# The last stage of a four-stage kernel, moved in blocks of 512 tokens into the steps of the third stage

## What is computed

```python
x = x + ln(windowed_attention(ln(x)))      # first stage,  "a"
x = x + ln(attention_and_8_experts(ln(x))) # second stage, "b"
x = x + ln(state_space_layer(ln(x)))       # third stage,  "c"
x = x + ln(mlp(ln(x)))                     # last stage,   "d"

def state_space_layer(x):                  # runs along the 256 tokens of a sequence
    x_ssm, z = split(ln(x) @ W_in)
    x_ssm = silu(causal_conv4(x_ssm)); dt = softplus(x_ssm @ dt_w + dt_b)
    h_t = exp(dt_t * A) * h_(t-1) + dt_t * x_t * B_t;  y_t = h_t @ C_t
    return x + ((y + x_ssm * D) * silu(z)) @ W_out

def mlp(x):                                # 128 -> 512 -> 512 -> 512 -> 128
    h = silu(x @ w1) * (x @ w2)
    h = gelu(h @ h1); h = gelu(h @ h2)
    return h @ w3
```

## Time and profile before

| what | value |
| --- | --- |
| median of 3 runs | 1017.56 us (1017.52 to 1021.14) |
| profiled execution, its own time | 1019.39 us |
| its span from first to last instruction | 1017.6 us |
| PE busy | 854.1 us, 84% |
| DVE busy | 680.2 us, 67% |
| ACT busy | 556.4 us, 55% |
| POOL busy | 459.0 us, 45% |
| chain that ended last, PE's share | 23% |
| granted TensorE clock, mean | 0.843 of full speed |

### The profile page before, as it was taken

One profiled execution on the slowest core, in us unless ns is written; L12 is line 12 of the kernel. 1 busy time (PEld: TensorE's weight loads), 2 busy tenths in 40 slices (PEclk: granted clock), 3 DMA queues, 4 the chain that ended last, 5 costly groups with the idle time before them and its releaser, 6 DMA issues. The chain is left out here.

```text
span 1017.6 us, 21550 instructions
## 1 busy us (share of the span) xinstructions
PE 854.1 (84%) x8256; PEld 704.6 (69%) x8256; DVE 680.2 (67%) x1965; ACT 556.4 (55%) x1050; POOL 459.0 (45%) x781
## 2 busy tenths in 40 slices
PE   4888755789999999989587887887579999999994
PEld 4777644668888888767455576665458878788783
DVE  4888954757888887652399999999772180551712
ACT  3554522346667676646478877786354363542630
POOL 2876852323646454444467777867540020020201
PEclk9877855559999999977789877788589999999997
DMA  8200002000000000000000000000000000000000
GB/s 283 94 18 12 24 17 66 25 1 2 2 2 2 2 3 2 1 2 1 0 1 2 1 1 1 1 1 1 1 1 1 1 21 1 1 22 1 16 6 21
DMA packets 22149, 16.76 MB, mean 16 GB/s; under 512 B 2576, under 2 KB 20376, under 8 KB 21792
## 3 DMA queue, kind: packets, MB, share of 16 engines
q1 hardware_dynamic: 21040, 14.77, 4.7%
q10 hardware_dynamic: 1008, 0.63, 0.2%
HBM read 11.20 MB, written 4.19 MB: 15 GB/s over the span
## 5 line engine op out<-in xcount | busy, mean ns | idle before, releaser
L118 POOL TENSOR_TENSOR d_ln_ve<-d_ln_mv,eps 128x4 f32<-128x4 f32 x16 | 3.2, 200 | 228.7 <-DVE d_ln_mv L112 228.7
L1421 PE MATMUL ps<-h_h,wh_h 128*128 128x512 f32 x256 | 99.7, 389 | 0.0
L1423 PE MATMUL ps<-h_l,wh_h 128*128 128x512 f32 x256 | 99.6, 389 | 0.0
L1422 PE MATMUL ps<-h_h,wh_l 128*128 128x512 f32 x256 | 99.6, 389 | 0.0
L1500 PE MATMUL ps<-w_e,he 128*128 128x128 f32 x512 | 87.0, 309 | 3.7 <-ACT he L690 3.4
L690 ACT ACTIVATE he<-ps,pp 128x256 f32<-128x256 f32 x128 | 59.7, 472 | 43.6 <-PE ps L1423 38.1
L1500 PEld LDWEIGHTS ps<-w_e,he 128*128 128x128 f32 x512 | 76.9, 221 | 6.1 <-ACT he L690 5.4
L1434 PEld LDWEIGHTS ps<-mov,hbd 32*128 32x128 f32 x2048 | 78.1, 232 | 0.0
L1434 PE MATMUL ps<-mov,hbd 32*128 32x32 f32 (+1 forms) x2048 | 77.2, 308 | 0.0
L1388 DVE TENSOR_TENSOR d_y<-ps,w_s 128x512 f32<-128x512 f32 x8 | 5.5, 692 | 103.0 <-PE ps L1857 103.0
L1354 DVE TENSOR_TENSOR h_l<-hid,h_h 128x512 fp32r<-128x512 f32 x64 | 48.5, 771 | 31.3 <-ACT h_h L921 30.4
(11 more groups left out here) (286 smaller groups left out, 2614.8 us busy)
## 6 DMA issues: line engine op xcount, KB each, us to landing
x<-in_x SPq DMA_DIRECT2D x16, 128.0 KB
w_h<-in_w_h SPq DMA_DIRECT2D x2, 1024.0 KB, 8.2
x<-x SPq DMA_DIRECT2D x16, 128.0 KB, 1.8
xB<-x SPq DMA_DIRECT2D x32, 64.0 KB
out_x<-xB SPq DMA_DIRECT2D x32, 64.0 KB
w_m<-in_w_m SPq DMA_DIRECT2D x3, 256.0 KB, 5.8
xB<-in_w_e SPq DMA_DIRECT2D x1, 512.0 KB
w_e<-in_w_e SPq DMA_DIRECT2D x1, 512.0 KB
```

Source lines behind the costliest of these rows:

```text
L1421: pe.matmul(dst, a_h, b_h, start=start, stop=True, skip_group_check=True)
L1422: pe.matmul(dst, a_l, b_h, start=False, stop=True, skip_group_check=True)
L1423: return pe.matmul(dst, a_h, b_l, start=False, stop=True, skip_group_check=True)
```

## The change

The last stage runs in 8 blocks (b = 0 to 7) of 512 tokens, one lane. Its work is put into `step_c` on every engine. `block_of(n, behind)` gives the block that a step works on: a block enters in step 2b + 4 (its norm, its turned tiles, gate and up of m = 0), is in the middle in step 2b + 5 (gate and up of m = 1 to 3, hidden layer 1), ends in step 2b + 6 (hidden layer 2, last product), and leaves in step 2b + 7 (output norm, addition). So from step 5 on the steps alternate: odd ones have a middle (and from 7 on a leaving) block, even ones an ending and an entering block. Blocks 0 to 5 end inside the third stage; block 6 enters in step 16, and `tail()` does the rest of block 6 and block 7.

The blocks use PSUM banks 6 and 7 alone: gate and up of one m take both, a hidden layer alternates between them. For that the pair products go through banks 4 and 5 in two halves (`pairs(t, k)`, `terms(t, k)`, k = 0, 1), and the B and C projections go to bank 5 (BC = 5). The products of the second half follow in the next step, behind `terms(n, 0)`. Lanes are gone: `raw`, `gate`, `d_xh`, `h0_h` and so on exist once. The weights are split in steps 0 to 4 (two of ten pieces a step, ACT `weight_heads`, POOL `low_parts`). The output norm of the third stage is done one step earlier. In the tail, other banks are used too. Every matmul of the last stage is still made, as many as before.

The diff, cut to its core:

```diff
-        IN, DT, BR, STATE, PAIRS, BC = 0, 1, 2, 3, 4, 7
+        IN, DT, BR, STATE, PAIRS, BC = 0, 1, 2, 3, 4, 5
...
+        def block_of(n, behind):
+            return (n - behind) // 2 if n >= behind and (n - behind) % 2 == 0 and n <= NB else None
...
         @block.scalar
...
+            def hidden1(b, m):
+                act.wait_ge(m_h1_ps, nth(b, m))
+                if m >= 2:
+                    act.wait_ge(m_h1, nth(b, m - 2))
+                chain.link(act.activation(raw[m % 2][:, :], ps[:, hidden_bank(b, 0, m), :], ACT.Gelu, scale=vec("h1_s", m)))
+                act.activation(h1_h[:, m, :], raw[m % 2][:, :], ACT.Copy).then_inc(m_h1_high, 1)
...
             def step_c(n, have):
...
                 if have(1):
                     log_part(n + 1)
+                if middle is not None:
+                    gated(middle, 0)
                 if have(0):
                     skip_path(n)
+                if middle is not None:
+                    high0(middle, 0)
+                    gated(middle, 1)
+                if ending is not None:
+                    hidden2(ending, 0)
...
+                if ending is not None:
+                    hidden2(ending, 2)
+                    hidden2(ending, 3)
+                if entering is not None:
+                    turned_tokens(entering)
                 if have(2):
                     silus(n + 2)
+                if middle is not None:
+                    gated(middle, 2)
...
+                    gated(middle, 3)
+                    high0(middle, 3)
                 if have(1):
                     decays(n + 1)
+                if middle is not None:
+                    hidden1(middle, 0)
...
+            def tail():
+                gated(b, 0)
+                output_norm(NB - 1)
+                gated(b, 1)
...
         @block.vector
...
+            def raised(b, m):
+                dve.wait_ge(m_gate, nth(b, m))
...
+                dve.scalar_tensor_tensor(out=raw[m % 2][:, :], in0=ps[:, up_bank(b, m) + 1, :], scalar=vec("w2_s", m),
+                                         in1=gate[m % 2][:, :], op0=ALU.mult, op1=ALU.mult).then_inc(m_raw, 1)
...
             def step_c(n, have):
+                if entering is not None:
+                    tokens_in(entering)
                 if have(2):
                     conv_input(n + 2)
+                if leaving is not None:
+                    tokens_out(leaving)
+                if ending is not None:
+                    low1(ending, 2)
+                    low1(ending, 3)
                 if have(0):
                     decay_products(n)
                 if have(-1):
                     from_states(n - 1)
-                if have(0):
-                    terms(n)
+                if middle is not None:
+                    raised(middle, 0)
+                if have(0):
+                    terms(n, 0)
...
+                if leaving is not None:
+                    output_normed(leaving)
                 if have(0):
                     carried(n)
...
                 if have(1):
                     inputs_by_chunk(n + 1)
+                if middle is not None:
+                    low0(middle, 3)
+                if n >= 4 and have(-1):
+                    residual(n - 1)
+                if have(0) and n >= 4:
+                    states(n)
+                if entering is not None:
+                    tokens_low(entering)
+                if ending is not None:
+                    scaled(ending)
...
         @block.tensor
...
-            def pairs(t):
+            def pairs(t, k):
...
-                    pe.wait_ge(S["c_term"], t)
-                for g in range(4):
-                    last = pe.matmul(ps[:, PAIRS + g, 0:BC_AT], ones[heads(g), :], prod[l][heads(g), :],
-                                     start=True, stop=True)
+                    pe.wait_ge(S["c_term"], 2 * t + k)
+                for g in range(2):
+                    part = heads(2 * k + g)
+                    last = pe.matmul(ps[:, PAIRS + g, 0:BC_AT], ones[part, :], prod[l][part, :], start=True, stop=True)
...
+            def gate_and_up(b, m):
+                if m == 0:
+                    pe.wait_ge(S["d_xl"], b + 1)
+                    if b >= 1:
+                        pe.wait_ge(S["d_yr"], min(b, LAST - 1))
+                elif b < LAST - 1:
+                    pe.wait_ge(m_raw, nth(b, m - 1))
...
+            def hidden(b, w, m):
+                src_h, src_l, ready, done = ((h0_h, h0_l, m_h0, m_h1_ps), (h1_h, h1_l, m_h1, m_h2_ps))[w]
+                if m == 0:
+                    pe.wait_ge(ready, nth(b, HID - 1))
+                elif m >= 2 and b < LAST - 1:
+                    pe.wait_ge((m_h1_high, m_h2)[w], nth(b, m - 2))
...
             def step_c(n, have):
                 if have(1):
                     in_and_out(n + 1)
                     step_size(n + 1)
                 if have(2):
                     turned_input(n + 2)
                 if have(-1):
                     from_states(n - 1)
+                if ending is not None:
+                    hidden(ending, 1, 0)
+                if have(0):
+                    pairs(n, 1)
                 if have(1):
                     outputs_by_chunk(n + 1)
+                if middle is not None:
+                    gate_and_up(middle, 1)
                 if have(2):
                     convolved(n + 2)
+                if middle is not None:
+                    gate_and_up(middle, 2)
+                if ending is not None:
+                    hidden(ending, 1, 1)
                 if have(0):
                     chunk_weights(n)
                 if have(1):
                     inputs_by_chunk(n + 1)
+                if middle is not None:
+                    gate_and_up(middle, 3)
+                if ending is not None:
+                    hidden(ending, 1, 2)
                 if have(0):
                     chunk_states(n)
+                if middle is not None:
+                    hidden(middle, 0, 0)
                 if have(-1):
                     projected(n - 1)
+                if ending is not None:
+                    hidden(ending, 1, 3)
+                if entering is not None:
+                    tokens_turned(entering)
                 if have(1):
-                    pairs(n + 1)
+                    pairs(n + 1, 0)
+                if middle is not None:
+                    hidden(middle, 0, 1)
+                if ending is not None:
+                    last_product(ending)
                 if have(0):
                     turned_states(n)
+                if middle is not None:
+                    hidden(middle, 0, 2)
+                    hidden(middle, 0, 3)
+                if entering is not None:
+                    gate_and_up(entering, 0)
```

More of the change, by code:

```diff
@@ L32 @@
 ITER = NB // 2
-ITER_MLP = NB // 4
 PP = {}
@@ L625, in _ @@
                     products(0)
[L626 removed]
+            for n in range(0, NB + 1):
                 step_c(n, within(n))
[L628 to L631 removed]
+            tail()
         @block.scalar
@@ L933, in _ @@
                 fill(n, 1)
-            for n in range(0, NB + 3):
+            for n in range(0, NB + 1):
                 step_c(n, within(n))
-                if n == NB - 1:
-                    step_d(-1, 0, within(-1, ITER_MLP))
-            for n in range(0, ITER_MLP + 1):
-                step_d(n, 0, within(n, ITER_MLP))
+            tail()
         @block.vector
@@ L1344, in step_c @@
                     inputs_by_chunk(n + 1)
+                if middle is not None:
+                    low0(middle, 3)
[7 more added lines that the diff above has]
+                    scaled(ending)
+                if n >= 4 and have(4):
+                    statistics(n + 4)
@@ new lines, in tail @@
+                low1(b, 3)
+                raised(c, 0)
+                raised(c, 1)
+                low0(c, 0)
+                low0(c, 1)
+                raised(c, 2)
+                raised(c, 3)
+                low0(c, 2)
+                low0(c, 3)
+                scaled(b)
+                tokens_out(b)
+                for m in range(HID):
+                    low1(c, m)
+                output_normed(b)
+                scaled(c)
+                tokens_out(c)
+                output_normed(c)
@@ L1863, in _ @@
             for n in range(-6, NB + 1):
                 step_b(n, n % 4, within(n))
-            pairs(0)
-            for n in range(0, NB + 3):
+            pairs(0, 0)
+            for n in range(0, NB + 1):
                 step_c(n, within(n))
-                if n == NB - 1:
-                    step_d(-1, 0, within(-1, ITER_MLP))
-            for n in range(0, ITER_MLP + 1):
-                step_d(n, 0, within(n, ITER_MLP))
+            tail()
 def lay_out(inp):
```

481 lines of the change are left out of this document (289 added, 192 removed).

## The result

The changed kernel takes 1097.66 us (median of 4 runs, 1091.74 to 1103.29), the kernel before 1018.39 in the same job: the ratio is 1.077, 95% interval 1.0745 to 1.0801. So it is slower by 79 us; 1058.8 was forecast, in a range from 1000 to 1085, and the measured time lies above it. The sign was right, the size (+41) was half of what came.

A forecast was written before the change was run, and what follows sets the result against it. DVE was taken to bound the third stage and PE the last. Step terms put the end of step 15 at 944.6 us; 114 for the rest gave 1058.8, +41 us, in a range from 1000 to 1085.

The forecast's parts named there:

- I take 1.2 a step, 4.8: Steps 0 to 3: DVE waits 0.65 us for the second half, 0.15 for two instructions, low clock up to 1.7.
- Costed at nothing: Work assumed free: most SP stores, POOL's extra norms, addition and weight splits, ACT's slack and table loads except the silu load.
- Step 4, 2.9: Step 4 adds statistics, norm and one wait for the half, less one set of statistics: 2.9 us more.
- Odd step 39.7: Four odd steps within 6 to 14: 35.7 us by the queue walk, plus 4 for PE's low clock.
- Step 5: First odd step with a middle block, no leaving block or last product ahead: 30 + 4 us.
- Step 15: Last step of the third stage, an odd one without the next tile's work: 31 + 4 us.
- Even step 27.25: Five even steps within 6 to 14: PE waits 1.6 us, then is full; states end at 27.25 us.
- The clock, +4.0 a pair: Two PE idle stretches in odd steps, 6.2 and 4.5 us, each followed by 4 us at half speed, 2 us lost.
- Tail, 114: From the end of step 15 to the end of the span: 114 us, with 2 us for the clock.
- The table load at 1.28 us, without a drain: ACT's table load priced at 1.28 us from the row; the skill's 2.66 with drain would give about 1075.
- Rival 3: Clock lower for longer, mean 0.80 in all of the pair: 6 x 4 us more, 1083; chance 0.13.
- Rivals 1, 2 and 4: PE becomes the bound, 957, chance 0.19; clock stays full, 1035, 0.2; waits and gain cancel within 5 us, 0.08.

The follow-up runs named there:

- the halves alone: The kernel before with only pairs and terms in two halves in all 16 steps, last stage left in place: 1068.27 us, ratio 1.0423.
- whole tiles: The changed kernel with the pair products of tiles 0 to 3 made in one go through four banks: 1083.04 us, ratio 1.058.
- the weights alone: The kernel before with only the last stage's weights split in steps 0 to 4 of the third stage: 1025.66 us, ratio 1.0007.
- Fillers: The changed kernel with 12 and 7 unread matmuls in PE's two idle stretches of odd steps 5 to 13: 1076.96 us, ratio 1.0503.

## Why the prediction was right in sign and short by 39 us

- *"I take 1.2 a step, 4.8", steps 0 to 3:* this step failed, and it is the first one. The half was priced as if it took half of the whole ("DVE waits 0.65"); it takes as long as the whole, 0.91, and 1.65 at the clock it meets. The prediction allowed up to 1.7 for the low clock and took 1.2. Shown by the halves alone: 3.1 us a step. In the changed kernel, whole tiles give back 13.6 us, of which 3.8 in step 0 and 9.0 in steps 1 to 3, where the prediction had 4.8: 8.0 us short.
- *"Costed at nothing", the weights:* failed. POOL had the time, but DVE did not have its own while POOL used it: 7.8 us in steps 1 to 4, shown by the weights alone. The time of that run (ratio 1.0007) hides it behind a shorter wait later; its trace shows both parts.
- *Step 4, 2.9:* the block's first work, with a half of its own, cost 4.8, so 1.9 short; the rest of the step is above. These three make up, to 0.1, the 17.8 us that steps 0 to 4 were short.
- *Odd step 39.7:* right in mechanism and order, both waits found (6.50 for 6.2, 3.58 for 4.5), 41.1 to 42.4 measured, so 7.4 us short over four of them. In step 9 the second half comes 1.1 us late, and the last product ahead of it ends at 5.7 for 5.2; no run took these small delays apart. *Step 5*, 34: 36.5. *Step 15*, 35: 36.8.
- *Even step 27.25:* 27.7 to 30.3, 8.6 us short over five; in two of them the clock fell behind a wait of 2 us, 1.7 us each, and the rest is small delays like the decay products' 3.90 for 3.2.
- *The clock, +4.0 a pair:* right. Fillers give 20.8 us in the five steps that have them, 4.2 each (23.8 in steps 5 to 15, 384.4 less 360.6); the term had 4.0 for each of six.
- *Tail, 114:* 112.2. The terms that are listed for it add up to about 98.1 where the prediction has 99.2, so part of the agreement is luck.
- *The table load at 1.28 us, without a drain:* right. In step 9 ACT's load starts at 753.09, takes 1.28 us, and the gate starts at 754.38.
- *0.2 from the end of matmuls to their reader:* more than the rows show, as the profile models these ends (762.20 to the gate at 762.23 in step 9), so it did not make the sum short.
- *Rival 3* (lower clock for longer, 1083) has part of the truth in the even steps. *Rivals 1, 2 and 4* fell: PE is at 80% from step 5 to 15, and the clock was low.

The terms from the walk through the queues held within 5% (full odd steps) and 7% (even steps) on average, but there are eleven such steps, and their small errors all go one way: 20.3 of the 36 us. No single step of the walk failed there. The two terms that were scaled or left out, half of an operation and a cover on another engine, carried 15.8 us in five steps.

## What to carry to other kernels

Interleaving two stages with opposite bounds need not make them shorter, when each then hands every piece of work on through two buffers: here a stage without waits on DVE and one with few on PE became a chain through three engines that takes longer than the two one behind the other, even with its clock and its order mended. Price a part of an operation by what limits it, not by its share of the work: matmuls in separate row strips took as long for two as for four here (0.91 and 0.93 us). An idle engine is not free cover if its work slows the one that bounds the stage (3.2 to 4.7 us here), so look at the neighbour's durations, not only at its own busy time, and never at the total alone, which can hide a loss behind a gain.

## What the runs showed of the hardware

- Two fp32 matmuls of 384 columns in two strips of 32 rows take 0.91 us, four in four strips 0.93; at a clock of 0.50 the two take 1.65.
- Waits of 6.5 and 3.6 us on PE lost some 4 us a pair of steps in the work behind them (clock 0.50 and 0.59); 12 and 7 matmuls with no reader in the two waits gave it back (clock 1.00). Behind a wait of 2.04 us the clock was 0.57 in step 10 and 1.00 in step 8. Where the clock was already low, two such matmuls changed nothing (2.02 us for 4 passes) and four cost more than the idle time they filled (3.73 for 8).
- DVE's seven decay products took 4.7 us instead of 3.2 while POOL subtracted two tiles of 128x512. What blocks them is not shown.
